# A 16-step ring in place of the 21-step tile loop of a fused cross-attention, self-attention and expert kernel

## The chip, the cores and the metric

The kernel runs on one core of a Trainium2 chip. The metric is the device time of one launch in microseconds (us). Five engines of the core have queues of their own and meet through semaphores: TensorE (PE in the profile), VectorE (DVE), ScalarE (ACT), GpSimd (POOL) and SyncE (SP), which here only issues transfers. Each engine works its queue strictly in the order in which the program wrote it, so an instruction that waits holds everything behind it on that engine.

## What is computed

The input x has 32 batches of 32 tokens with 256 features, and the context 32 batches of 257 rows with 64 features. Three layers follow each other, all in 32-bit accuracy:

```python
x = x + xattn(layernorm(x), ctx)      # 16 heads, softmax over 257 context rows, rotary embedding on ctx
x = x + attn(layernorm(x), wq, wk, wv, wo)   # 16 heads of 128, softmax over 32 tokens, block-scaled weights
x = x + ffn(layernorm(x))             # 64 experts, top 8 of them per token, at most 128 tokens each
```

## The kernel before

The 1024 tokens are cut into T = 8 tiles of 128 tokens, which are 4 batches each. The kernel has a fold stage (it multiplies the weights of the first layer together), the tile loop, and an expert stage. The change touches the tile loop alone.

**Three tiles at once.** In `tile(i, j, m)` the first layer runs for tile i ("X work"), the second for tile j = i - 1 ("S work"), and the output projection, the router and the scatter to the experts for m = j - 1. A tile has STEPS = 21 steps. ROWS = 16 of them each begin a "row": the scores of one batch and 4 heads (128 x 257, two f16 matmuls, L1188 and L1189, `score_row`). A row then passes through the negated maximum on VectorE (L830, `max_row`), the exponential on ScalarE (L609, `exp_row`), a transposition on TensorE two steps later (L1196, `transpose_row`), a copy on ScalarE (L617, `copy_row`) and the weighted sum on TensorE three steps later (L1207, `sum_row`). Scores have two PSUM banks, the transposed rows one, the sums of the RB = 4 rows of a batch share one. `normalise` on VectorE (L836 to L840) adds the part of context row 257, which GpSimd has prepared (L479, `last_rows`), and divides.

**Items between the rows.** The tables X_AT and BEHIND name what else stands in each step. X items: `hT` transposes the normalised tile, `qa` and `qb` make its queries (L1161; ScalarE casts them to f16 at L588, VectorE computes the f16 remainder at L824), `kt0` to `kt3` transpose the context of a batch (L1166, L592, L820), `cT0` to `cT3` transpose the normalised sums (L1171, L597), and `out` is the projection (L1175), which VectorE adds to X (L847). S items: `hT`, `q0` to `k3` (split f16 matmuls L1142 to L1144, drained by VectorE at L867), `sc` (scores, L1234; shifted on VectorE at L872 and L873, exponential on ScalarE at L638), `v0` to `v3` (drained by ScalarE, L630), `pv0` to `pv3` (L1244, drained at L634 and L883), `wo0` to `wo3`, `rT`, `log` and `pos`. Between `sc` and `pv0` lie the sum of the softmax (`softmax_sum`, L854), its end and transposition (`softmax_end`, L858 and L859) and four copies into a block-diagonal matrix on ScalarE (`spread`, L648). `chosen` (L903 to L907), `weigh` and `place` (L919 to L921) are the router's work on VectorE. The X items take turns on two PSUM banks, the S items on two others: an item may start when the item two places before it on the list XS or SS has been drained.

**The seam.** The rows fill steps 0 to 15. Steps 16 to 20 have no new row: they hold `qa`, `qb`, `cT3`, `kt0` and `out`, of which `qa`, `qb`, `kt0` belong to tile i + 1, and `score_row` of the next tile waits for `qb` and `kt0` before its first row. GpSimd runs a loop of its own: `rope_products` for tile i + 1 (L456 to L461), then for each batch `last_rows` and `rope_sums` (L471), and the scatter of tile m, 8 indirect transfers, at the end.

**The first tile** also carries 11 of the 16 parts in which the second layer's weights are dequantised (L769 on VectorE, L564 on ScalarE, L503 on GpSimd), in steps 0 to 15.

The order of the sums of a new batch is held by this line of `sum_row`, for the first row of the batch:

```python
e.wait_ge(on_ready, i * BT + b)      # normalise of the batch before has finished all three operations
```

## Time and profile before

| what | value |
|---|---|
| median of 3 runs | 779.98 us (776.14 to 783.31) |
| the profiled execution | 785.1 us, of which span 783.3 us |
| busy PE / DVE / ACT / POOL | 79% / 54% / 37% / 38% of the span |
| fold stage, until about | 78 us |
| tile loop | 78 to 629 us |
| expert stage | 629 to 783 us |

The profile is one execution. "Busy" counts the time in which an engine has an instruction in work; matmuls overlap, each is shown about 0.16 us longer than its place in the queue, so a short wait can hide in the busy time. "PEclk" is the granted clock of TensorE as a share of 2.4 GHz, 0.50 is 1.2 GHz. In the tables below, the stretches are cut where the projection `out` of a tile ends: 144.9 us for tile 0, then 199.9, 256.0, 317.6, 379.1, 440.6, 502.7 and 554.9 us.

### The profile page before, as it was taken

The numbers are of one execution on the slowest core, as the hardware profiler recorded it, in microseconds if no ns is written. First come the engines' busy times: TensorE is split into PE (matmuls) and PEld (weight loads), VectorE is DVE, ScalarE is ACT, GpSimd is POOL, SyncE is SP. The second block draws the span as 40 slices with busy tenths as digits, with TensorE's granted clock in tenths as the row PEclk, the third lists the DMA queues.
The fourth block names the chain that finished last, engine by engine and source line by source line (L and its number), as shares of the span: only waits on it lengthen the run. The fifth ranks groups of instructions, "written<-read, shape, count | busy, mean of one in ns | idle before, by whom it ended". The sixth has DMA issues, their size and how long they took to land.

```text
span 783.3 us, 16249 instructions
## 1 busy us (share of the span) xinstructions
PE 622.6 (79%) x6211; PEld 534.6 (68%) x6211; DVE 426.4 (54%) x1091; ACT 288.1 (37%) x798; POOL 294.7 (38%) x279
## 2 busy tenths in 40 slices
PE   6995677898999987898899798898874178898860
PEld 4884566797877876787787696796753067777750
DVE  1255485465676675676576577577653323333334
ACT  1123364337346345236236236246031033333320
POOL 3113299211214414313412412400303337777780
PEclk9975567999999999999999999999999579999995
DMA  7946993999001101100100200100101069999988
GB/s 200 293 140 156 237 251 84 294 338 300 6 2 53 38 3 54 35 3 34 55 3 18 72 2 2 69 2 2 66 2 51 28 167 284 301 301 296 303 168 275
DMA packets 98987, 97.61 MB, mean 125 GB/s; under 512 B 26238, under 2 KB 92848, under 8 KB 98912
## 3 DMA queue, kind: packets, MB, share of 16 engines
q1 hardware_dynamic: 86016, 78.21, 34.2%
q0 software_dynamic: 12288, 17.95, 10.5%
q8 instruction: 51, 0.84, 0.4%
q10 hardware_dynamic: 608, 0.42, 0.2%
q14 instruction: 24, 0.20, 0.1%
HBM read 62.32 MB, written 35.19 MB: 124 GB/s over the span
## 4 chain that ended last, share of the span: by engine, by line
PE 43%; DVE 20%; issue 13%; ACT 9%; POOL 6%; DMA 6%; another core or an unknown queue 2%; SPq 0%; POOLq 0%; DVEq 0%; PEldq 0%; ACTq 0%
POOL expert_sums L545 6%; PE bank L1161 5%; PE bank L1175 5%; PE bank L1142 5%; PE bank L1144 4%; PE bank L1143 4%; PE bank L1207 4%; DMA expert_sums<-Wh,etok 3%; PE bank L1244 3%; ACT pr L609 2%; DVE nmax L830 2%; PE bank L1196 2%; ACT diag L648 2%; ACT space L630 2%
## 5 line engine op out<-in xcount | busy, mean ns | idle before, releaser
L545 POOL DMA_INDIRECT expert_sums<-Wh,etok x64 | 98.8, 1544 | 37.8 <-issue 22.5
L609 ACT ACTIVATE pr<-bank,nmax 128x257 f32<-128x257 f32 x128 | 61.0, 477 | 101.4 <-DVE nmax L830 101.0
L1142 PE MATMUL bank<-space,Wh 128*128 128x128 f16 x512 | 88.3, 219 | 9.9 <-DVE X L928 7.1
L488 POOL DMA_INDIRECT expert_rows<-h,slot x64 | 62.7, 980 | 87.5 <-DVE slot L921 70.4
L1143 PE MATMUL bank<-space,Wh 128*128 128x128 f16 x512 | 88.2, 219 | 0.0
L1144 PE MATMUL bank<-space,Wl 128*128 128x128 f16 x512 | 88.2, 219 | 0.0
L1207 PE MATMUL bank<-Cr,pT 128*128 128x64 f32 x512 | 77.0, 276 | 9.4 <-DVE On L840 8.4
L471 POOL TENSOR_TENSOR Cr<-C,Ct 128x192 f32<-128x192 f32 x64 | 41.7, 675 | 104.9 <-PE bank L1207 104.8
L1207 PEld LDWEIGHTS bank<-Cr,pT 128*128 128x128 f32 x512 | 72.4, 204 | 12.4 <-issue 11.1
L830 DVE TENSOR_REDUCE nmax<-bank 128x1 f32<-128x257 f32 x128 | 53.3, 418 | 42.8 <-PE bank L1189 40.6
L479 POOL TENSOR_TENSOR On<-Cr,pr 128x256 f32<-128x256 f32 x32 | 20.7, 647 | 138.4 <-ACT pr L609 138.4
L1345 PE MATMUL bank<-Wh,ring 128*96 128x128 f32 x512 | 68.1, 277 | 0.0
L617 ACT COPY pT<-bank 128x256 f32<-128x256 f32 x128 | 47.6, 372 | 43.0 <-PE bank L1196 42.3
L1142 PE MATMUL bank<-Wh,space 128*128 128x256 f16 (+1 forms) x192 | 59.2, 309 | 4.8 <-ACT space L630 3.3
L867 DVE SCALAR_TENSOR_TENSOR space<-bank,bqk 128x512 f32<-128x512 f32 x64 | 43.5, 689 | 33.1 <-PE bank L1144 33.0
L1345 PEld LDWEIGHTS bank<-Wh,ring 128*96 128x96 f32 x512 | 60.9, 166 | 0.4 <-issue 0.3
L1196 PE MATMUL bank<-ident,pr 128*128 128x128 f32 x256 | 52.6, 289 | 10.5 <-ACT pT L617 10.5
L1142 PEld LDWEIGHTS bank<-space,Wh 128*128 128x128 f16 x512 | 51.1, 100 | 13.0 <-DVE X L928 8.2
L1143 PE MATMUL bank<-Wl,space 128*128 128x256 f16 (+1 forms) x192 | 59.1, 308 | 0.0
L1144 PE MATMUL bank<-Wh,space 128*128 128x256 f16 (+1 forms) x192 | 59.1, 308 | 0.0
L1354 PE MATMUL bank<-ring,Wh 96*128 96x256 f32 x128 | 43.4, 420 | 13.4 <-DVE Wh L1031 9.9
L1143 PEld LDWEIGHTS bank<-space,Wh 128*128 128x128 f16 x512 | 50.1, 98 | 0.1
(175 smaller groups left out, 1401.0 us busy)
## 6 DMA issues: line engine op xcount, KB each, us to landing
ring<-L_ffn_gate_up_proj_dram SPq DMA_DIRECT2D x64, 192.0 KB
expert_rows<-h SPq DMA_DIRECT2D x8, 1284.0 KB, 15.7
Wh<-expert_rows SPq DMA_DIRECT2D x64, 160.5 KB
ring<-L_ffn_down_proj_dram SPq DMA_DIRECT2D x64, 96.0 KB
expert_sums<-h SPq DMA_DIRECT2D x4, 1152.0 KB, 13.4
C<-ctx_dram SPq DMA_DIRECT2D x24, 128.0 KB, 3.3
Wl<-expert_sums SPq DMA_DIRECT2D x3, 1024.0 KB, 6.9
space<-L_xattn_Wo_dram SPq DMA_DIRECT2D x8, 256.0 KB, 4.8
```

The lines of the kernel that those rows point to most:

```text
L488: e.indirect_dma_start(XE[:, :], bass.IndirectOffsetOnAxis(ap=slot[:, k:k + 1], axis=0), h3[:, :], None, bounds_check=E * CAP - 1, oob_is_ ...
L545: e.indirect_dma_start(Y[n % NY][:, :], bass.IndirectOffsetOnAxis(ap=etok[:, n % 4:n % 4 + 1], axis=0), ye[:, n % 4], None, bounds_check=Y ...
L609: e.activation(pr[:, s, :], bank[r % 2][:, 0:NL], ACT.Exp, bias=nmax[:, s:s + 1], accum_out=rsum[:, s:s + 1]).then_inc(expd, 1)
L617: e.copy(pT[:, r % 2], bank[2][:, 0:2 * P].rearrange("p (c t) -> p c t", c=2)).then_inc(pt_ready, 1)
L830: e.tensor_reduce(nmax[:, s:s + 1], bank[r % 2][:, 0:NL], AX.X, ALU.max, negate=True).then_inc(maxed, 1)
L867: e.scalar_tensor_tensor((qS, kS)[w][:, 4 * g:4 * g + 4, :], src[:, :].rearrange("p (h t) -> p h t", h=4), 1.0 / WS, bqk[:, w, 4 * g:4 * g ...
L1142: e.matmul(dst, ah, bh, start=first and n == 0, stop=False)
L1143: e.matmul(dst, ah, bl, start=False, stop=False)
L1144: ins = e.matmul(dst, al, bh, start=False, stop=last and n == len(terms) - 1)
L1196: ins = e.transpose(bank[2][:, c * P:(c + 1) * P], pr[:, r % (2 * RB), c * P:(c + 1) * P], ident[:, :])
L1207: ins = e.matmul(bank[3][:, o:o + DC], pT[:, r % 2, c, :], Cr[:, b, c, 0, :], start=c == 0, stop=c == 1)
L1345: ins = e.matmul(bank[2 + n % 2][0:I, half * P:(half + 1) * P], gu[:, n, c, half * I:(half + 1) * I], xeT[:, n % 2, c, :], start=c == 0, s ...
```

## The change

The 21-step tile with its seam becomes a ring of 16 steps, in which a row starts in every step, over the tile border too. Step n = 16 g + t works on row t of tile g; there are 165 steps in all.

- **X items.** `hT`, `kt0`, `qa`, `qb` of tile g + 1 stand in steps 11, 12, 13 and 15 of tile g, in the order hT, kt0, qa, qb; `cT3` and `out` of tile g - 1 in steps 3 and 4 of tile g. `score_row` waits for `qa` before row 0 and for `qb` before row 2.
- **S items.** The S work of a tile begins in step 5 and ends in step 3 of the next turn. `wo0` and `wo1`, `q0` and `q1`, `q2` and `q3`, `pv0` and `pv1`, `pv2` and `pv3` share steps.
- **VectorE.** `chosen` stands behind the S item of its step (with `sc` in step 13, before it stood one step ahead of `sc`); `pos` stands behind `softmax_sum`, `place` ahead of the `pv` items.
- **sum_row.** The first row of each batch is issued at the end of its step, behind the X and S items, and waits only for the first addition of `normalise` (`x_link`), no longer for all three operations.
- **GpSimd.** `rope_products` stands in step 5, behind the scatter (step 4); the parts of tile 0 stand in the step of their number, the clearing of `diag` in step 9 of tile 1.
- **Waits moved.** VectorE's wait for the blanked expert rows (`own_tokens`) goes from the start of tile 2 to its step 10.

```diff
-XS = ["kt1", "kt2", "cT0", "kt3", "cT1", "cT2", "hT", "qa", "qb", "cT3", "kt0", "out"]
-X_AT = {2: ["kt1"], 6: ["kt2"], 7: ["cT0"], 10: ["kt3"], 11: ["cT1"], 15: ["cT2", "hT"], 16: ["qa"], 18: ["qb"],
-        19: ["cT3", "kt0"], 20: ["out"]}
+XS = ["kt1", "cT3", "out", "kt2", "cT0", "kt3", "cT1", "hT", "kt0", "qa", "qb", "cT2"]
+XTILE = {"cT3": -1, "out": -1, "hT": 1, "kt0": 1, "qa": 1, "qb": 1}
+X_AT = {2: ["kt1"], 3: ["cT3"], 4: ["out"], 6: ["kt2"], 7: ["cT0"], 10: ["kt3"], 11: ["cT1", "hT"], 12: ["kt0"],
+        13: ["qa"], 15: ["qb", "cT2"]}
...
-BEHIND = {0: ["wo0"], 1: ["wo1"], 2: ["wo2"], 3: ["hT", "wo3"], 4: ["q0"], 5: ["q1"], 6: ["q2", "q3"], 7: ["k0", "rT"],
-          8: ["k1", "k2", "log"], 9: ["k3"], 10: ["sc"], 11: ["v0", "pos"], 12: ["v1"], 13: ["v2"], 14: ["v3"],
-          15: ["pv0"], 16: ["pv1"], 17: ["pv2"], 18: ["pv3"]}
-STEPS = ROWS + 5
+S_FIRST = 5
+S_AT = {5: ["wo0", "wo1"], 6: ["wo2"], 7: ["hT", "wo3"], 8: ["q0", "q1"], 9: ["q2", "q3"], 10: ["k0"],
+        11: ["rT", "k1", "k2"], 12: ["log", "k3"], 13: ["sc"], 14: ["v0"], 15: ["pos", "v1"], 0: ["v2"], 1: ["v3"],
+        2: ["pv0", "pv1"], 3: ["pv2", "pv3"]}
+ALL_STEPS = ROWS * (T + 2) + S_FIRST
...
 # GpSimd
+            def step(g, t):
+                j, m = turn_of(g, t)
+                if t == 0 and 1 <= g <= T:
+                    last_rows(g - 1, 3)
+                if t == 3 and 1 <= g < T:
+                    rope_sums(g, 3)
+                if t == 4 and g < T:
+                    last_rows(g, 0)
+                if t == 4 and m is not None:
...
+                    scatter(m)
+                if t == 5 and g + 1 < T:
+                    rope_products(g + 1)
+                if t in (7, 11, 15) and g + 1 < T:
+                    rope_sums(g + 1, t // 4 - 1)
+                if t in (8, 12) and g < T:
+                    last_rows(g, t // 4 - 1)
...
 # VectorE
+            def step(g, t):
+                n = ROWS * g + t
+                j, m = turn_of(g, t)
+                if g < T:
+                    max_row(g, t)
+                if t % RB == 2 and RB + 2 <= n and n - RB - 2 < T * ROWS:
+                    normalise(*divmod((n - RB - 2) // RB, BT))
+                for name in X_AT.get(t, ()):
+                    if name in XSPLIT and 0 <= g + XTILE.get(name, 0) < T:
+                        x_low(name, g + XTILE.get(name, 0))
...
+                for name in S_AT.get(t, ()):
...
+                        s_use(name, j)
+                if j is not None and t == 14:
+                    softmax_sum(j)
+                if j is not None and t == 15:
+                    softmax_end(j)
+                if m is not None and t == 13:
+                    chosen(m)
...
 # TensorE, score_row and sum_row
-                if r == 0:
-                    wait_pos(e, xd, xpos("qb", i))
+                if r in (0, 2):
+                    wait_pos(e, xd, xpos("qb" if r else "qa", i))
...
-                if r % RB == 0:
-
-                    e.wait_ge(on_ready, i * BT + b)
+                if r % RB == 0 and i * BT + b >= 1:
+
+                    e.wait_ge(x_link, 2 * (i * BT + b) - 1)
...
+            def step(g, t):
+                if g < T:
+                    score_row(g, t)
+                row = row_of(ROWS * g + t - 2)
+                if row:
+                    transpose_row(*row)
+                row = row_of(ROWS * g + t - 3)
+                if row and row[1] % RB:
+                    sum_row(*row)
+                if g <= T:
+                    for name in X_AT.get(t, ()):
+                        x_item(name, g)
+                for name in S_AT.get(t, ()):
+                    s_item(name, *turn_of(g, t))
+                if row and row[1] % RB == 0:
+                    sum_row(*row)
```

**TensorE at the tile border.** Before, from `sum_row` of row 13 (step 16) to the first row of the next tile: L1161 is `qa` and `qb`, L1244 a `pv` item, L1171 `cT3`, L1166 `kt0`, L1175 `out`, L1188 the scores.

```order
L1207 MATMUL bank<-Cr,pT 128x64 x2
L1161 MATMUL bank<-h1T,M 128x128 x8
L1244 MATMUL bank<-diag,space 128x128 x4
L1196 MATMUL bank<-ident,pr 128x128 x2
L1207 MATMUL bank<-Cr,pT 128x64 x2
L1244 MATMUL bank<-diag,space 128x128 x4
L1207 MATMUL bank<-Cr,pT 128x64 x2
L1161 MATMUL bank<-h1T,M 128x128 x8
L1244 MATMUL bank<-diag,space 128x128 x4
L1171 MATMUL bank<-ident,On 128x128 x2
L1166 MATMUL bank<-ident,Cr 128x128 x3
L1175 MATMUL bank<-N,cT 128x256 x8
```

No scores stand in this stretch: it is the seam. After, steps 2 to 4 of the ring: L1151 is `kt1`, L1230 the `pv` items, L1156 `cT3`, L1160 `out`, L1174 and L1175 the scores, L1182 and L1193 transposition and sum.

```order
L1193 MATMUL bank<-Cr,pT 128x64 x2
L1151 MATMUL bank<-ident,Cr 128x128 x3
L1230 MATMUL bank<-diag,space 128x128 x8
L1174 MATMUL bank<-KTh,qspace 128x257
L1175 MATMUL bank<-KTl,qspace 128x257
L1182 MATMUL bank<-ident,pr 128x128 x2
L1156 MATMUL bank<-ident,On 128x128 x2
L1230 MATMUL bank<-diag,space 128x128 x8
L1193 MATMUL bank<-Cr,pT 128x64 x2
L1174 MATMUL bank<-KTh,qspace 128x257
L1175 MATMUL bank<-KTl,qspace 128x257
L1182 MATMUL bank<-ident,pr 128x128 x2
```

The queries and `kt0` have left this place, rows have come in, and the first sum of the batch (the last L1193) stands behind the `pv` items.

**VectorE between the scores of the S work and its softmax.** Before, from `sc` (L872) to the end of the softmax (L859); L830 is a row's maximum, L896 to L899 `pos`.

```order
L872 TENSOR_REDUCE smax<-bank 128x16
L873 TENSOR_TENSOR space<-bank,smax 128x512
L830 TENSOR_REDUCE nmax<-bank 128x1
L896 TENSOR_TENSOR sv<-bank,slot 128x64
L897 SCALAR_TENSOR_TENSOR sv<-bank,sv 128x64
L899 TENSOR_TENSOR count<-count,mask 128x64
L854 TENSOR_REDUCE ssum<-space 128x16
L855 RECIPROCAL sinv<-ssum 128x16
L830 TENSOR_REDUCE nmax<-bank 128x1
L858 TENSOR_TENSOR space<-space,sinv 128x512
L859 STREAM_TRANSPOSE space<-space 128x512
```

Only a row's maximum and `pos` stand between `sc` and the sum. After, from the remainder of `qa` (L819) through `sc` (L867, L868), `chosen` (L898 to L902), a row's maximum (L825), `normalise` (L831 to L835) and `softmax_sum` (L849, L850) to the next row's maximum:

```order
L819 TENSOR_TENSOR qspace<-bank,qspace 64x4x4x32 x2
L867 TENSOR_REDUCE smax<-bank 128x16
L868 TENSOR_TENSOR space<-bank,smax 128x512
L898 CAST topf<-topi 128x8
L899 TENSOR_TENSOR space<-iota_e,topf 128x512
L902 TENSOR_REDUCE mask<-space 128x64
L825 TENSOR_REDUCE nmax<-bank 128x1
L831 TENSOR_TENSOR On<-bank,On 128x256
L834 RECIPROCAL rinv<-rsum 128x4
L835 TENSOR_TENSOR On<-On,rinv 128x256
L849 TENSOR_REDUCE ssum<-space 128x16
L850 RECIPROCAL sinv<-ssum 128x16
```

Behind these rows follow the remainder of `qb` (L819), `pos` (L891 to L894), and only then the end of the softmax (L853, L854).

## Rows read from the trace of the kernel before

**Rows 1.** Busy time by stretches, us: PE, PEld, DVE, ACT, POOL, clock, DMA

```profile
145.00:199.90 54.90, 51.22 (x627) 45.34 (x625) 32.26 (x72) 26.26 (x75) 12.20 (x17) 1.00 0.92 297
199.90:256.00 56.10, 51.60 (x634) 45.60 (x633) 38.91 (x102) 27.42 (x79) 16.57 (x20) 1.00 0.06 22
256.00:317.60 61.60, 53.73 (x635) 46.47 (x633) 39.58 (x102) 27.14 (x79) 20.30 (x26) 0.97 0.12 36
440.60:502.70 62.10, 53.72 (x635) 46.86 (x633) 41.44 (x102) 27.22 (x79) 19.05 (x23) 0.97 0.07 25
502.70:554.90 52.20, 47.40 (x597) 41.60 (x596) 34.68 (x96) 24.53 (x73) 7.49 (x10) 1.00 0.04 14
```

**Rows 2.** Waits of PE from 379.1 to 440.6: us, times, longest

```profile
PE bank L1166 <- DVE qspace L824: 2.5, 1, 2.5
PE bank L1207 <- DVE On L840: 1.3, 1, 1.3
PE bank L1142 <- DVE X L928: 1.3, 1, 1.3
PE bank L1220 <- DVE h L811: 1.1, 1, 1.1
```

**Rows 3.** Stretches at the seam, columns as in rows 1

```profile
250.00:256.00 6.00, 4.42 (x25) 3.61 (x24) 2.50 (x4) 1.78 (x4) 4.74 (x5) 1.00 0.38 140
370.00:374.00 4.00, 1.29 (x9) 0.84 (x8) 2.07 (x3) 1.71 (x4) 3.08 (x4) 1.00 0.36 134
375.00:376.00 1.00, 1.00 (x4) 0.77 (x3) 0.43 (x1) 0.01 (x1) 0.98 (x2) 0.50 0.45 164
```

**Rows 4.** Timeline of PE, items: start, us, [idle before]

```profile
252.32 3.69 PE L1175 MATMUL bank<-N,cT 128*128 128x256 f32 x16
...
367.35 2.00 PE L1161 MATMUL bank<-h1T,M 128*128 128x128 f32 x16
...
373.73 5.38 PE L1175 MATMUL bank<-N,cT 128*128 128x256 f32 x16 [0.94 <-issue]
```

**Rows 5.** Timeline of DVE, operations of one step each

```profile
408.07 1.10 DVE L907 TENSOR_REDUCE mask<-space 128x64 bf16<-128x512 f32 x1
...
409.55 0.41 DVE L836 TENSOR_TENSOR On<-bank,On 128x256 f32<-128x256 f32 x1
...
410.89 0.68 DVE L872 TENSOR_REDUCE smax<-bank 128x16 f32<-128x512 f32 x1
...
413.77 0.69 DVE L854 TENSOR_REDUCE ssum<-space 128x16 f32<-128x512 f32 x1
...
414.77 0.42 DVE L830 TENSOR_REDUCE nmax<-bank 128x1 f32<-128x257 f32 x1
...
426.93 1.39 DVE L824 TENSOR_TENSOR qspace<-bank,qspace 64x512 f16<-64x512 f32 x2 [0.82 <-ACT qspace L588]
```

**Rows 6.** Timeline of ACT, operations of one step each

```profile
417.36 1.24 ACT L648 COPY diag<-space 32x512 f32<-32x512 f32 x2
418.62 0.60 ACT L630 ACTIVATE space<-bank 128x512 f32<-128x512 f32 x1
...
425.73 1.17 ACT L588 CAST qspace<-bank 64x512 f16<-64x512 f32 x2 [1.59 <-PE bank L1161]
```

**Rows 7.** Timeline of DVE: one operation of the norm's chain, in two tiles

```profile
204.30 0.16 DVE L744 TENSOR_TENSOR rs<-rs 128x1 f32<-128x1 f32 x1
...
384.23 1.35 DVE L744 TENSOR_TENSOR rs<-rs 128x1 f32<-128x1 f32 x1
```

**Rows 8.** Timeline of POOL at that time

```profile
383.76 1.81 POOL L461 TENSOR_TENSOR C<-C,cosT 128x768 f32<-128x768 f32 x1
```

**Rows 9.** Timeline of PE at the start of tile 0

```profile
78.65 6.64 PE L1161 MATMUL bank<-h1T,M 128*128 128x128 f32 x32 [0.55 <-ACT h1T L597]
87.98 0.91 PE L1166 MATMUL bank<-ident,Cr 128*128 128x128 f32 x3 [2.69 <-DVE qspace L824]
89.81 0.40 PE L1188 MATMUL bank<-KTh,qspace 128*128 128x257 f16 x1 [0.93 <-DVE KTl L820]
```

More of the change, by code:

```diff
@@ L692, in expert_copy @@
+            e.sem_inc(x_high, XSPLIT.index("kt0"))
+            for name in XS:
+                if XTILE.get(name, 0) == 1:
+                    x_use(name, 0)
+            for n in range(ALL_STEPS):
+                step(n // ROWS, n % ROWS)
             def expert_copy(ex, n):
@@ L1011, in _ @@
             next_h1(0)
-            for name in ("qa", "qb", "kt0"):
-                x_low(name, 0)
-            tile(0, None, None)
-            tile(1, 0, None)
-            e.wait_ge(zero_out, 16 * (E // 8 + NY))
-            e.tensor_scalar(h3[:, D + E:ROW], h3[:, D + E:ROW], float(-(B * S + P)), None, ALU.add).then_inc(zeroed, 1)
-            e.wait_ge(zeroed, 3)
-            for j in range(1, T - 2):
-                tile(j + 1, j, j - 1)
-            tile(T - 1, T - 2, T - 3, last=True)
-            tile(None, T - 1, T - 2)
-            tile(None, None, T - 1)
+            for name in XSPLIT:
+                if XTILE.get(name, 0) == 1:
+                    x_low(name, 0)
+            for n in range(ALL_STEPS):
+                step(n // ROWS, n % ROWS)
+            assert all(done[which, i] == count for which, count in (("x", XLINKS), ("s", SLINKS), ("r", RLINKS))
+                       for i in range(T)), done
             def experts(j, first):
@@ L1322, in _, with x_item @@
-            for name in XS:
-                (x_use(name, 0) if name in XNEXT else x_skip(name, -1))
-            tile(0, None, None)
-            tile(1, 0, None)
-            for j in range(1, T - 2):
-                tile(j + 1, j, j - 1)
-            tile(T - 1, T - 2, T - 3, last=True)
-            tile(None, T - 1, T - 2)
-            tile(None, None, T - 1)
+            def x_item(name, g):
+                i = g + XTILE.get(name, 0)
+                if 0 <= i < T:
+                    x_use(name, i)
+                else:
+                    x_skip(name, i)
@@ L1333, in expert_t @@
+            for name in XS:
+                x_item(name, -1)
+            for n in range(ALL_STEPS):
+                step(n // ROWS, n % ROWS)
             def expert_t(j, n):
```

251 lines of the change are left out of this document (99 added, 152 removed).

## The prediction

> **What bounds the kernel now.** I read the page first: TensorE is busy 79% of the span, no other engine over 54%. Then the busy time by stretches, cut where `out` of a tile ends [rows 1]. Tiles 3 to 6 take 61.6, 61.5, 61.5 and 62.1 us, 246.7 together, and TensorE is busy for 53.7 of each. Tile 2 has the same work (634 matmul records against 635) and takes 56.1, with 51.6 busy. So a full tile is bound by TensorE's queue with 51.6 us of work, plus what it waits, plus something that makes the same work 2.1 us longer. The waits of a steady tile are the third view [rows 2]: 2.5 us for the remainder of the queries, 1.3 for the division of the batch before, 1.3 for X, 1.1 for h; four short ones, 1.6 us together, bring it to 7.8, as 61.5 - 53.7 asks. The longer work is the clock: at the seam TensorE idles 2.7 us of 370 to 374, and at 375 it is granted 0.50, which is 1.2 GHz [rows 3]. The sixteen matmul records of `out` then take 5.38 us instead of 3.69 (which holds `kt0` too) [rows 4]. I count 1.8 us a tile. In tile 2 it idles 1.6 us at this place and the clock stays 1.00 [rows 3].
>
> By the Trainium skill (TensorE: Matmul & The Clock Gate, HAM oscillation) a TensorE that pauses too long is put back to half its clock and pays for it at the next burst. The trace agrees: 0.50 right behind the gap.
>
> **What the ring takes away.** The 2.5 us for the query remainder and the pause before `out` go: `qa` and `qb` stand in steps 13 and 15 and are wanted in steps 0 and 2, several us of TensorE work later; `cT3` and `out` have two `pv` items and a sum between them. The 1.3 us for the division go: the first sum stands behind the items and waits for one operation of three. With the gap at the seam the fall of the clock there goes, 1.8 us.
>
> **What it adds.** No instruction of weight is added. The order is what changes, so I walk one period with the rows' durations, TensorE's own pieces being scores 0.22, transposition 0.22, sum 0.39, query item 1.84, `sc` 1.2, a `v` item 1.3 (starts of neighbours in the timeline). The bad place is `sc`. Behind the last matmul of `qa` (time 0) come, each waiting for the one before: cast of `qa` on ScalarE 1.2 [rows 6], its remainder on VectorE 1.3, as the queue is in order [rows 5]: 2.5. Only then maximum and shift of `sc`, 2 x 0.7: 3.9. `chosen`, 0.2 + 0.7 + 1.1: 6.0. Row maximum and `normalise`, 0.35 + 1.0: 7.4. `softmax_sum`, 1.0: 8.4. The maximum of row 15, its exponential and the cast of `qb` on ScalarE, 0.35 + 0.5 + 1.2: 10.5. Its remainder 1.3, `pos` 0.7, the end of the softmax 1.4: 13.9. Maximum and exponential of row 0, 0.9, then ScalarE's queue: two pairs of `spread` at 1.25, `v2` 0.5, the copy of row 15 0.25, exponential 0.5, `v3` 0.6 [rows 6]: 19.2 when `pv0` may start. TensorE has in that time `sc` 1.2, steps 14, 15, 0 and 1 with 2.1 + 4.3 + 2.1 + 2.1, and 1.2 of step 2: 13.0. So 6.2 us of waits lie between `qa` and `pv0`, in five pieces: the transposition of row 13 for the copy of row 12, which stands behind the exponential of `sc` (1.6), `cT2` (0.4), `v2` for `pos` (2.0), the transposition of row 0 (1.0), `pv0` (1.2). Before, none of `qa`, `qb`, `chosen` stood in this chain.
>
> The rest of the period: `hT` of the S work. From the end of `out` VectorE does a maximum, X and its norm (3.5 us), then `normalise` and the remainder of `kt2`, then the second half of the norm: h is there at 7.5, TensorE at 6.6: 1.0. The first `q` waits for X 0.8 (before 1.3), `rT` and `k` 1.4 together, since `self_out_norm` now stands behind `normalise`. Sum 6.2 + 3.2 = 9.4. The profile hides 0.16 us of each of the eight, so it would show 8.2 idle. Then GpSimd: the same small product of the norm takes 0.16 us in one tile and 1.35 in another [rows 7], where it ends with the GpSimd operation beside it [rows 8]. In the ring `rope_products` comes behind ten us of scatter, about 6 to 10 us behind `out`, again on the second half of that norm. I take 0.5. The two bounds are 0 and the 1.2 us of the rows.
>
> The Trainium skill (GPSIMD Engine Reference, Specifications) says that VectorE and GpSimd share an SBUF interface when VectorE reads two SBUF tensors. By that the product can be held each time it meets a `rope` operation, 1.2 us in every tile and the sum below 4 us dearer. The trace shows both cases.
>
> **The sum, against the profiled 783.3 us.** A full tile of the ring: 51.6 + 8.2 + 0.5 = 60.3 us.
> - Tiles 3 to 6: 4 x 60.3 = 241.2 against 246.7: -5.5.
> - Tile 2: 59.8 (its `rope_products` is early, as now) against 56.1: +3.7. It never lost its clock.
> - Tile 1 has no router work; without `chosen` and `pos` the chain is 2.9 us shorter. 51.2 busy, idle 3.7: 54.9, as now: 0.
> - Tile 7 has no queries to make and 5 of its 16 rows have moved ahead (0.83 each, 4.2 us): 47.4 - 4.2 + 6.7 idle (3.2 as above, 3.5 around `sc`) = 49.9 against 52.2: -2.3.
> - Tile 0: `kt0` before the queries. Now it waits 2.69 us behind them and the first row starts at 89.8 [rows 9]; in the new order the 32 records of the queries end at 85.3 and row 0 can go: -4. At its end the five rows that moved in fill the seam but GpSimd, behind which the last batch stands, is busy with parts: +1. Together -3.
> - Behind tile 7 the order is the same but for `chosen` and `place`: 0. Expert stage: 0.
>
> Sum -7.1. The profiled execution took 785.1 us, the median is 780.0; I set the change against the median: 773.
>
> **Rivals.**
> A (forecast, 0.42): as above, 768 to 778.
> B: the clock falls at the new gaps (0.2). In step 2 TensorE works 0.2, waits 1.0, works 0.9, waits 1.2; that is less idle than the 2.7 us behind which it fell and more than tile 2's 1.6, behind which it did not [rows 3]. One fall costs 1.8 in each of tiles 2 to 6, 9 us: 782, no change.
> C: the ring is better than my walk (0.25). Each wait rests on a chain of ten durations, and if VectorE gets `chosen` or `normalise` done while ScalarE casts, two us a tile go in tiles 1 to 6, -12: 761. For it: VectorE is busy only 41 of 62 us [rows 1]. Against it: its queue is in order and `qa`'s remainder waits at its head.
> D: slower (0.13). The clock falls twice in a period, at `v2` and at `pv0`, 3.6 us in each of tiles 2 to 6, and GpSimd's hold is the full 1.2: 18 + 3 - 7 = +14: 794. It decides the case if two gaps of a period are each followed by a granted clock of 0.50; with one of them it is B.
>
> The rule of the page cited first is what B and D rest on: by it the time would be 782 or 794. The trace so far bears it out at the seam alone.
>
> **How the numbers follow.** About 1% is what a measurement of this kernel tells from no change, 772 to 788. A lies across the lower bound: I give a third of it to faster. Faster: 0.14 + 0.24 (C) = 0.38. Slower: D, 0.12 with a bit of B, 0.15. Same 0.47. The range reaches from C, 761, with 3 us below it, to the end of B: 758 to 787. It leaves out D and the far end of C, 2 in 10.
>
> **What the profile after would show.** Right: steady tiles near 60 us; no wait for the query remainder before `kt0`; no wait of the weighted sum for the division; `out` in 3.7 us at clock 1.00; new waits of `v2`, `pv0` and row transpositions of 1 to 2 us each; first row near 85.5 us; tile 2 longer than 56.1. Wrong: tiles of 57 or less (then the chain behind `qa` is shorter than walked), 0.50 in the clock behind step 0 or 2 (B, D), or a wait of GpSimd's `last_rows` behind the scatter, which I cost at nothing since `normalise` of batch 1 comes 8 us later.

## The result and the profile after

The changed kernel takes 828.6 us (819.8 to 830.2, 4 runs) beside 781.6 us (776.1 to 789.1, 4 runs) of the kernel before: ratio 1.060, 95% interval 1.049 to 1.072. A second timing gave 827.6 beside 780.0, ratio 1.056 (1.046 to 1.066). The forecast was 773, with a range to 787. The profiled execution took 830.0 us (span 828.1); it is set against the 783.3 us of the trace before.

By stretches, cut where `out` ends as before (150.7, 213.3, 274.6, 342.4, 409.9, 477.5, 544.4, 601.8 us):

| stretch | before | after | forecast |
|---|---|---|---|
| to the end of tile 0 | 145.0 | 150.7 | 142.0 |
| tile 1 | 54.9 | 62.6 | 54.9 |
| tile 2 | 56.1 | 61.3 | 59.8 |
| tiles 3 to 6, each | 61.5 to 62.0 | 66.9 to 67.8 | 60.3 |
| tile 7 | 52.3 | 57.3 | 49.9 |
| the rest, to the end | 228.4 | 226.4 | 228.4 |

The busy time of three of them (columns as in [rows 1]), tiles 1, 2 and 5:

```profile
150.70:213.30 62.60, 53.74 (x627) 47.38 (x625) 34.07 (x71) 26.60 (x75) 15.68 (x19) 0.95 0.85 271
213.30:274.60 61.30, 51.91 (x635) 45.69 (x633) 39.80 (x103) 27.19 (x79) 10.72 (x16) 1.00 0.05 13
409.90:477.50 67.60, 56.91 (x635) 48.43 (x633) 40.60 (x102) 27.14 (x79) 18.70 (x24) 0.92 0.08 27
```

Tile 2 is the ring as I walked it, 51.9 busy and 9.4 idle at full clock. Tile 5 has the same work and a scatter besides, is 6.3 us longer, and runs at 0.92. TensorE's waits in tile 5, against [rows 2]:

```profile
PE bank L1206 <- DVE h L806: 2.7, 2, 1.7
PE bank L1156 <- DVE On L835: 2.0, 2, 1.8
PE bank L1127 <- DVE sv L892: 1.9, 1, 1.9
PE bank L1182 <- ACT pT L624: 1.7, 1, 1.7
PE bank L1230 <- ACT space L637: 0.8, 1, 0.8
```

The waits at the seam are gone. The last three of these are those walked (1.9 for `pos`, 1.7 for the copy of row 12, 0.8 before `pv0`). The longer ones of the first two, 1.7 for h and 1.8 for `cT0`, lie 8 to 12 us behind `out`, and there something else happens. ScalarE, then VectorE, then the transposition on TensorE that the copy L624 waits for, in the order of time:

```profile
411.05 0.20 ACT L616 ACTIVATION_READ_ACCUMULATOR pr<-bank,nmax 128x1 f32 x1
417.33 0.37 ACT L624 COPY pT<-bank 128x256 f32<-128x256 f32 x1 [6.08 <-remote]
```
```profile
412.75 0.16 DVE L736 SCALAR_TENSOR_TENSOR rs<-rs 128x1 f32<-128x1 f32 x1
417.37 0.43 DVE L825 TENSOR_REDUCE nmax<-bank 128x1 f32<-128x257 f32 x1 [4.46 <-remote]
417.71 0.42 DVE L831 TENSOR_TENSOR On<-bank,On 128x256 f32<-128x256 f32 x1
418.16 0.18 DVE L834 RECIPROCAL rinv<-rsum 128x4 f32<-128x4 f32 x1
418.37 1.51 DVE L835 TENSOR_TENSOR On<-On,rinv 128x256 f32<-128x256 f32 x1
```
```profile
413.44 0.38 PE L1182 MATMUL bank<-ident,pr 128*128 128x128 f32 x2
```

Both stand still and go on within 0.04 us of each other. "Remote" says that the profile shows nobody who released them. Not all of the 6.08 and 4.46 us is the stop: ScalarE could not copy before the transposition ended at 413.8, VectorE could not take the maximum before the scores ended at 413.6. In tile 2 the same copy waits 2.6 us for TensorE and starts 0.04 us behind the transposition:

```profile
216.85 0.38 PE L1182 MATMUL bank<-ident,pr 128*128 128x128 f32 x2
217.27 0.37 ACT L624 COPY pT<-bank 128x256 f32<-128x256 f32 x1 [2.61 <-PE bank L1182]
```

In tile 5 it starts 3.5 us behind it, and the maximum 3.8 us behind its scores (0.1 in tile 2). That is the stop. In tiles 3 to 7 it is 3.4 to 3.7 us on ScalarE and 3.7 to 3.9 on VectorE. GpSimd at that time, first and last of the eight transfers and what follows:

```profile
405.80 1.01 POOL L500 DMA_INDIRECT expert_rows<-h,slot  x1 [0.18 <-issue]
...
414.78 0.97 POOL L500 DMA_INDIRECT expert_rows<-h,slot  x1 [0.30 <-issue]
415.77 1.00 POOL L468 TENSOR_TENSOR Ct<-C,sinT 128x384 f32<-128x384 f32 x1
416.71 1.00 POOL L470 TENSOR_TENSOR Ct<-C,sinT 128x384 f32<-128x384 f32 x1
417.79 1.80 POOL L473 TENSOR_TENSOR C<-C,cosT 128x768 f32<-128x768 f32 x1
```

Here the stop ends about when the scatter's data has landed (its last packets start at 416.9). The division L835, which takes 0.42 us in tile 7, where no rope operation runs, and 0.85 in tile 2, takes 1.51 beside `rope_products`. TensorE then:

```profile
418.00:422.00 4.00, 0.67 (x4) 0.22 (x3) 3.75 (x11) 0.93 (x4) 2.80 (x3) 0.88 0.00 0
422.00:426.00 4.00, 3.82 (x19) 3.11 (x20) 0.79 (x3) 1.10 (x4) 0.62 (x1) 0.50 0.00 0
```

It works 0.67 of 4 us and is then granted 0.50, 1.2 GHz. ScalarE's wait of 6.0 to 6.2 us, with the stop in it, stands in each of tiles 3 to 7, the five that have a scatter under rows, and not in tile 2. It is no wait for instructions to arrive, as far as the trace tells: no packet of the instruction queues starts between 410.2 and 430.5.

### The profile page after: what moved, and what is told of

Its sections match the earlier page's. It is cut to its first block, busy times and chain, and to the rows that moved or that the text cites. A ratio compares the mean times of both kernels' runs of the same rounds, so it can differ in the third digit from the quotient of the medians.

```text
span 828.1 us, 16290 instructions
## 1 busy us (share of the span) xinstructions
PE 641.5 (77%) x6211; PEld 544.4 (66%) x6211; DVE 428.8 (52%) x1091; ACT 287.8 (35%) x798; POOL 292.3 (35%) x279
## 4 chain that ended last, share of the span: by engine, by line
PE 42%; DVE 23%; issue 12%; ACT 7%; DMA 7%; POOL 6%; another core or an unknown queue 2%; SPq 0%; POOLq 0%; DVEq 0%; PEldq 0%; ACTq 0%
PE bank L1127 5%; PE bank L1129 5%; PE bank L1128 5%; DMA expert_sums<-Wh,etok 4%; POOL expert_sums L557 4%; PE bank L1193 4%; PE bank L1160 4%; PE bank L1230 3%; DVE qspace L819 2%; PE bank L1146 2%; DVE On L835 2%; ACT qspace L600 2%; PE bank L1116 2%; PE bank L1104 2%
## 5 line engine op out<-in xcount | busy, mean ns | idle before, releaser
L483 POOL TENSOR_TENSOR Cr<-C,Ct 128x192 f32<-128x192 f32 x64 | 38.4, 622 | 180.3 <-PE bank L1193 175.9
L624 ACT COPY pT<-bank 128x256 f32<-128x256 f32 x128 | 47.6, 372 | 148.4 <-PE bank L1182 117.5
L1127 PE MATMUL bank<-space,Wh 128*128 128x128 f16 x512 | 90.1, 222 | 7.3 <-DVE obias L932 2.7
L616 ACT ACTIVATE pr<-bank,nmax 128x257 f32<-128x257 f32 x128 | 61.1, 477 | 84.8 <-DVE nmax L825 83.9
L1128 PE MATMUL bank<-space,Wh 128*128 128x128 f16 x512 | 89.8, 221 | 0.0
L825 DVE TENSOR_REDUCE nmax<-bank 128x1 f32<-128x257 f32 x128 | 53.2, 418 | 68.4 <-PE bank L1175 49.6
L1193 PE MATMUL bank<-Cr,pT 128*128 128x64 f32 x512 | 79.3, 282 | 0.0
L1193 PEld LDWEIGHTS bank<-Cr,pT 128*128 128x128 f32 x512 | 77.0, 214 | 1.7 <-issue 0.3
L1182 PE MATMUL bank<-ident,pr 128*128 128x128 f32 x256 | 54.0, 296 | 29.6 <-ACT pT L624 29.3
L1127 PE MATMUL bank<-Wh,space 128*128 128x256 f16 (+1 forms) x192 | 64.1, 334 | 13.5 <-DVE sv L892 9.3
L1334 PE MATMUL bank<-Wh,ring 128*96 128x128 f32 x512 | 67.7, 276 | 0.1
L1129 PE MATMUL bank<-Wh,space 128*128 128x256 f16 (+1 forms) x192 | 64.7, 337 | 1.5 <-issue 1.5
L1128 PE MATMUL bank<-Wl,space 128*128 128x256 f16 (+1 forms) x192 | 64.5, 336 | 1.7 <-issue 1.7
L1334 PEld LDWEIGHTS bank<-Wh,ring 128*96 128x96 f32 x512 | 60.6, 166 | 0.6 <-issue 0.5
L1182 PEld LDWEIGHTS bank<-ident,pr 128*128 128x128 f32 x256 | 33.7, 153 | 39.2 <-issue 37.2
L1127 PEld LDWEIGHTS bank<-space,Wh 128*128 128x128 f16 x512 | 51.4, 100 | 11.4 <-DVE X L923 3.4
## 6 DMA issues: line engine op xcount, KB each, us to landing
expert_rows<-h SPq DMA_DIRECT2D x8, 1284.0 KB, 15.6
```

The lines of the kernel that those rows point to most:

```text
L616: e.activation(pr[:, s, :], bank[r % 2][:, 0:NL], ACT.Exp, bias=nmax[:, s:s + 1], accum_out=rsum[:, s:s + 1]).then_inc(expd, 1)
L624: e.copy(pT[:, r % 2], bank[2][:, 0:2 * P].rearrange("p (c t) -> p c t", c=2)).then_inc(pt_ready, 1)
L825: e.tensor_reduce(nmax[:, s:s + 1], bank[r % 2][:, 0:NL], AX.X, ALU.max, negate=True).then_inc(maxed, 1)
L1127: e.matmul(dst, ah, bh, start=first and n == 0, stop=False)
L1128: e.matmul(dst, ah, bl, start=False, stop=False)
L1129: ins = e.matmul(dst, al, bh, start=False, stop=last and n == len(terms) - 1)
```

## Experiments

The last two columns are of the profiled execution: the mean of tiles 3 to 6, and from the end of tile 7 to the end. "Before" is the kernel before in the same comparison. A row without a ratio is a single execution.

| label | us | before | ratio | tiles 3-6 | rest |
|---|---|---|---|---|---|
| before | 781.6 | | | 61.7 | 228.4 |
| after | 828.6 | 781.6 | 1.060 | 67.5 | 226.4 |
| ring_no_scatter | 779.5 | 785.3 | 0.993 | 61.1 | 212.6 |
| before_no_scatter | 749.8 | 785.3 | 0.955 | 56.3 | 212.8 |
| ring_half_scatter | 787.2 | 785.3 | | 61.2 | 221.8 |
| ring_early_scatter | 811.0 | 785.3 | 1.039 | 63.9 | 226.6 |
| ring_split_scatter | 794.4 | 764.9 | 1.039 | 61.2 | 223.3 |
| ring_paired_scatter | 785.4 | 764.9 | | 61.1 | 226.3 |
| ring_plain_scatter | 785.0 | 764.9 | | 61.1 | 219.6 |
| before_split_scatter | 767.3 | 764.9 | 1.005 | 57.9 | 224.2 |
| before_again | 777.8 | 780.0 | | 60.0 | 230.1 |
| ring_again | 827.6 | 780.0 | 1.056 | 67.6 | 229.3 |
| ring_short_chain | 799.5 | 780.0 | 1.013 | 59.9 | 225.8 |
| before_split_sum | 782.7 | 780.0 | 1.001 | 59.7 | 228.6 |
| ring_shorter_chain | 774.8 | 759.8 | 1.023 | 58.9 | 227.0 |
| ring_paired_again | 792.6 | 759.8 | 1.047 | 61.1 | 226.2 |
| before_split_again | 768.0 | 759.8 | 1.015 | 57.5 | 225.0 |
| ring_six_scatter | 799.3 | 759.8 | | 64.0 | 223.0 |
| before_third | 763.9 | 768.4 | | 56.4 | 228.0 |
| before_paired_scatter | 762.0 | 768.4 | 1.001 | 56.9 | 225.6 |

The kernel before is itself near 782 us in three of the comparisons and near 764 in the other three. So times are only read beside their own "before", and tiles from the traces. The number of the chip does not tell the two kinds apart: the record has chip 13 both at 764.9 and at 780.0.

**1. The scatter left out.** In `scatter` (shortened here; the waits for the scatter's end go too), and with `range(4)` and `range(6)` in place of the cut in the half and the six one:

```
-                for k in range(TOPK):
-                    e.indirect_dma_start(XE[:, :], ..., h3[:, :], ...).then_inc(scat, 16)
```

> The changed kernel with the eight indirect transfers of each scatter left out, so the expert stage reads blanked rows; all waits on the scatter's end are gone, everything else stands. Theory S (the scatter under the rows is what makes the ring slow: ScalarE, VectorE and TensorE resume together at 417.3 us when its data has landed, TensorE then drops to 0.50): tiles 3 to 6 fall from 67.5 us to the 61.2 of tile 2, which has no scatter, tile 7 from 57.4 to about 53, about 30 us in all: near 798 us. Theory Q (the queues' order alone makes the tile long: the chain behind qa and the norm, with or without the scatter): tiles 3 to 6 stay above 65, the kernel above 815 us. Rival C (it is only the clock that falls): tiles about 64, TensorE's granted clock 1.00 in place of 0.92 to 0.97, and the wait of ScalarE for the row's transposition still there at 6 us.

> The kernel before with the same eight transfers left out: what the scatter costs behind the seam. Theory S: it cost something there too, less, since at the seam only out and kt0 stand in its way: tiles 3 to 6 fall from 61.6 us towards the 56.1 of tile 2, at most 5.5 each, so between 755 us (all of it) and 775 us. If S is wrong (tile 2 is short for want of its router transfers' neighbours, not of the scatter): within 1% of before, 782. The difference of ring and before without any scatter is the cost of the ring proper: by my walk it should be near 0; what is left of the 47 us is then not the scatter's.

> The changed kernel with four of the eight transfers of each scatter left out (half of the chosen experts get no row). Tells whether the stall has the length of the scatter. Theory S with a stall that lasts until the scatter's data has landed: the three engines resume near 412 us in the frame of the full kernel, 5 us sooner, before or just as VectorE comes to the second half of the norm, and the stall of ScalarE shrinks from 6 us to about 1; tiles 3 to 6 near 62 to 63. If the stall hangs on something that only begins at the fourth or fifth transfer or on the first one alone: 6 us as before, tiles at 67, or none.

> The changed kernel with two of the eight transfers of each scatter left out. With four a steady tile took 61.3 us, with eight 67.5. If each transfer behind the fourth costs the same, because the other engines stand still while it runs: 64.4. If there is a threshold at five (one stall of fixed length, until the data of all has landed): the stall ends 2.5 us sooner, 65. If it is only the last two: 61.3.

Without a scatter the ring's tiles 3 to 6 are all 61.1 us, those of the kernel before 56.3. Theory S holds for what the scatter costs under the rows: 6.4 us a tile, 5.7 in tile 7. Behind the loop it costs 13.8 in the ring and 15.6 before, which no expectation had, so both times came out lower than expected (779.5 for 798, 749.8 for 755 to 775). Theory Q holds for the rest, since the ring is still 4.8 us a tile longer than before without any scatter, and 29.7 us longer as a whole (1.040). So the scatter is not the main part of the change's loss: it cost the kernel before 5.4 us a tile as well, and of the 5.8 us by which the ring's tiles 3 to 6 are longer, 4.8 are there without it. Rival C falls: here is a tile of 61.0 at a clock of 0.97, as long as tile 2 at 1.00; the ring waits for its chain, and a fall of the clock is paid out of waiting.

```profile
207.10:268.30 61.20, 51.81 (x634) 45.59 (x633) 39.80 (x103) 27.21 (x79) 10.75 (x15) 1.00 0.03 8
390.50:451.50 61.00, 53.28 (x634) 46.30 (x633) 39.75 (x102) 27.21 (x79) 10.16 (x15) 0.97 0.03 8
```

Four transfers cost nothing in the tiles. Six cost 2.9 us, near the 64.4 of a price for each transfer, but not by a stop: ScalarE's copy starts 0.04 us behind its transposition in every tile. (This was run where the kernel before took 760, see 3.) `rope_products` comes two transfers sooner and meets the norm's first half; this is VectorE in `ring_six_scatter`, with GpSimd's last transfer and `rope_products`:

```profile
399.24 0.27 DVE L734 TENSOR_SCALAR rs<-rs,mv 128x1 f32<-128x1 f32 x1
399.55 2.46 DVE L736 SCALAR_TENSOR_TENSOR rs<-rs 128x1 f32<-128x1 f32 x1
...
403.05 1.10 DVE L835 TENSOR_TENSOR On<-On,rinv 128x256 f32<-128x256 f32 x1
...
404.41 0.26 DVE L734 TENSOR_SCALAR rs<-rs,mv 128x1 f32<-128x1 f32 x1
404.70 0.46 DVE L736 SCALAR_TENSOR_TENSOR rs<-rs 128x1 f32<-128x1 f32 x1
```
```profile
399.03 0.97 POOL L500 DMA_INDIRECT expert_rows<-h,slot  x1 [0.30 <-issue]
400.00 1.03 POOL L468 TENSOR_TENSOR Ct<-C,sinT 128x384 f32<-128x384 f32 x1
400.95 1.03 POOL L470 TENSOR_TENSOR Ct<-C,sinT 128x384 f32<-128x384 f32 x1
402.06 1.81 POOL L473 TENSOR_TENSOR C<-C,cosT 128x768 f32<-128x768 f32 x1
403.95 1.19 POOL L483 TENSOR_TENSOR Cr<-C,Ct 128x192 f32<-128x192 f32 x2
```

L736, 0.16 elsewhere, took 2.46 and ended with the second operation of `rope_products`; L835 took 1.10 where tile 2 of the ring has 0.85. Part of that time is spent waiting anyway: h is 1.9 us later behind `out` than without a scatter (9.6 for 7.7). Tile 6, at full clock, is 1.8 us longer; the other three lie at 0.95 to 0.97 and are 2.9 to 3.5 longer. Beside L483 the instruction L734, whose operands in SBUF are one tensor and a column of factors, keeps its 0.26 while L736 behind it takes 0.46. The trace agrees there with the Trainium skill (GPSIMD Engine Reference, Specifications), which has the shared interface contended by VectorE instructions with two SBUF inputs.

**2. The scatter in other places.** Early: the step of `scatter` is 3, ahead of `last_rows`, in place of 4. Split and paired (`turn` is the tile of step 4):

```
-                if t == 4 and m is not None: scatter(m)
+                if t == 3: scatter(m, range(0, 4))      # split;  paired: range(0, 2)
+                                                        #         paired: t == 4, behind last_rows: range(2, 4)
+                if t == 6: scatter(turn, range(4, 8))   # split;  paired: range(4, 6), and t == 7: range(6, 8)
```

The code is shortened; the last tile's second half is issued behind the loop. Plain: each `indirect_dma_start` is a `dma_start` of `h3` to 128 consecutive rows.

> The changed kernel, all of its work, with the scatter in GpSimd's queue in step 3 ahead of last_rows, where it now stands in step 4 behind it: it begins at about 401 us in place of 405.8 and its data has landed by 412.5. Theory S: the stall moves to 408 to 412, behind out, where VectorE has X and its norm to do from PSUM that is already filled; rope_products end at 415 in place of 419.6 and no longer meet the norm's second half. 2 to 4 us per tile less in tiles 3 to 7, 10 to 20 in all: 810 to 818 us. Theory Q: the same time within 0.5%, or slower, as last_rows of batch 0 now comes 5 us later. Rival: the stall costs the same wherever the rows run beside it: 828.

> The changed kernel, all of its work, with each scatter cut in two: four transfers in step 3, ahead of last_rows, and four in step 6, behind rope_products, so that GpSimd does about 5 us of other work between them. Without a scatter a steady tile took 61.06 us, with four transfers 61.3, with eight 67.5: the first four cost 0.2, the next four 6.2. Theory B (a backlog: the stall comes only when more than four or five transfers follow each other): both halves are free, tiles 3 to 6 at 61.3 to 62, 785 to 792 us. Theory P (place: what stalls is what TensorE does 5 us and more after batch 1 has begun, whoever is running; the second half lies in that place, about 5 to 10 us later than in the full kernel): tiles at 65 to 67, 810 to 828 us.

> As the split one, but in pairs: two transfers each in step 3, step 4 behind last_rows, step 6 behind rope_products and step 7 behind rope_sums, with 0.6 to 4 us of GpSimd's other work between them, eight transfers within some 19 us. Theory B with a backlog that drains between pairs: tiles at 61.3, as with four transfers. If the backlog is counted over a longer time than these gaps give, or if the price is one of the transfers' number: tiles at 64 to 67.

> The changed kernel with each of the eight indirect transfers replaced by a plain one on the same queue, in the same place, that writes the same 128 rows of 1284 bytes to consecutive places (so the rows land at the wrong experts). It tells the bytes from the way they are addressed. If it is the bytes, or the number of transfers in the queue, that stalls the other engines: ScalarE still waits 6 us for the transposition, tiles 3 to 6 at 66 to 68. If it is the work of GpSimd on the rows' addresses, or the scattered writes: no such wait, tiles at 61 to 62.5, below 795 us.

Early gains 3.5 us a tile, within what S expected, and "remote" waits of 0.9 to 3 us on ScalarE move with the scatter. Split, paired and plain are at 60.9 to 61.4 in all of tiles 3 to 6, as if there were no scatter. That fits theory B, a backlog of more than four indirect transfers in a row, and a cost that is not one of bytes. It doesn't show either: these three, and the six transfers of 1, were run where the kernel before took 760 to 765, and the next section shows that the stop can be absent there anyway. What speaks for B in comparisons that did have the stop are `ring_half_scatter` (a single execution) and, below, the pairs of `ring_short_chain` and the halves of `before_split_sum`: none shows it in tiles 3 to 6. For plain transfers, and for six, there is no such run.

**3. The two kernels again.**

> The kernel before, unchanged, for a trace of its own beside the next three. In the last comparison it took 764.9 us where it had taken 785.3 in the one before, and before_split_scatter was no faster than it. Two readings: the stall behind the scatter differs from chip to chip (then the tiles 3 to 6 here are 57 to 58 us where the time is near 765, 61.5 where it is near 782, and the waits of ScalarE at the seam are there only in the second case), or the whole execution was quicker, the fold and expert stages too, with tiles of 61.5 all the same.

> The changed kernel, unchanged. If the stall is there in this comparison (before near 782): tiles 3 to 6 at 67.5 and 828 us, ratio 1.06. If it is not (before near 765): tiles at 61.1 to 61.5, about 787, and the ratio is that of the ring proper, 1.03. If the stall comes with the ring alone and the kernel before was only quicker by chance: 828 beside 765.

> The kernel before, unchanged. Its time was near 782 us in three comparisons and near 762 in two others, and no trace is at hand from the second kind. If this one is of the second kind (below 770) its trace shows where the 20 us are: tiles 3 to 6 at 57 us with TensorE's clock at 1.00 and the scatter all the same (then the stall at the seam is what differs), or tiles as long as in the first traces and shorter fold and expert stages. If it is near 780 it adds nothing but a third set of tiles: 58 to 61.6.

`ring_again` repeats the first trace: 67.5, 67.5, 67.5 and 67.7, with the same 6.1 us on ScalarE. `before_third` is the key to my mistake. It has the seam and eight transfers in one piece, and its tiles 3 to 6 take 56.7, 56.0, 56.3 and 56.7. The seam in it:

```profile
362.83 0.38 PE L1171 MATMUL bank<-ident,On 128*128 128x128 f32 x2
364.78 0.44 PE L1166 MATMUL bank<-ident,Cr 128*128 128x128 f32 x2 [1.57 <-DVE qspace L824]
...
365.17 3.62 PE L1175 MATMUL bank<-N,cT 128*128 128x256 f32 x16
```
```profile
362.70:366.70 4.00, 2.43 (x16) 2.01 (x15) 2.50 (x4) 1.83 (x5) 3.08 (x4) 1.00 0.36 132
366.70:370.70 4.00, 4.00 (x29) 3.46 (x28) 1.18 (x3) 0.56 (x2) 2.79 (x4) 1.00 0.31 114
```

And the same place in the trace of [rows 3, 4], where `out` took 5.38 us:

```profile
372.48 0.58 ACT L634 CAST space<-bank 128x512 f16<-128x512 f32 x1 [1.72 <-remote]
373.21 0.37 ACT L597 COPY cT<-bank 128x256 f32<-128x256 f32 x1
374.64 0.38 ACT L592 CAST KTh<-bank 128x257 f16<-128x257 f32 x1 [1.05 <-remote]
```

The same instructions in the same order, with GpSimd's transfers at the same place; only where ScalarE is stopped does TensorE's pause grow from 1.6 to 2.7 us and the clock fall. So the 5 us by which tiles 3 to 6 exceeded tile 2 before were the scatter's stop and the clock behind it, and not what the seam costs alone. The stop is a different one here: two, of 1.7 and 1.1 us, and the second ends at 374.6, while the scatter still has 96 packets to go, so the landing of the data is not what ends it. And a seam whose own pause is longer can lose the clock with no scatter at all. This is the seam of tile 0 in `before_third`, before the first scatter, and the clock is 0.73 from 140.0 to 145.3:

```profile
139.79 0.90 PE L1166 MATMUL bank<-ident,Cr 128*128 128x128 f32 x3 [2.41 <-DVE qspace L824]
140.48 4.82 PE L1175 MATMUL bank<-N,cT 128*128 128x256 f32 x16
```

In `before_no_scatter` the same wait, 2.39, is followed by an `out` of 3.62 at clock 1.00: a pause of that length can be followed by either.

**4. The chain behind `qa`.** VectorE's queue in steps 12 to 15, on the paired ring:

```
 step 12:  log, k3                                      + chosen            (shorter)
 step 13:  maximum, qa's remainder, sc, chosen          -> maximum, sc, qa's remainder
 step 14:  ..., softmax_sum                             + chosen            (short)
 step 15:  maximum, qb's remainder, pos, softmax_end    -> maximum, softmax_end, pos, qb's remainder
```

> All of the ring's work, the scatter in pairs as in ring_paired_scatter (steady tiles 61.1 us, 9.2 of them idle), and VectorE's queue behind qa in another order: the scores' maximum and shift ahead of qa's remainder, chosen behind softmax_sum, softmax_end ahead of pos and of qb's remainder. By the walk of the prediction the end of the softmax comes 3.7 us sooner and pv0 could start 15.5 us behind qa in place of 19.2, with 13 us of TensorE work between. Theory Q (this chain is the price of the ring over before, 61.1 against 56.0 to 57.6 us): tiles 57.5 to 58.5, waits for the copy of row 12, for pos and before pv0 together under 3 us in place of 6. If the idle time is only passed on (the queries' remainder now late for row 0, or chosen late for pos): 60 to 61.

> ring_short_chain with chosen one step further ahead, at the end of step 12, in the 2.8 us that VectorE spends waiting for the cast of qa. In ring_short_chain a steady tile took 59.5 us and the 3.6 us of waits for pos and the copy of row 12 had become 2.5 us for chosen's mask. Theory Q (the chain behind qa is the ring's price): that wait goes as well, 0 to 0.5 is left of it, tiles 57 to 57.7, about 12 us less than ring_short_chain over tiles 2 to 7 and 20 less than ring_paired_scatter. Rival (the idle time goes round: TensorE waits for whoever is last, and pv0 or h takes it up): 59 to 59.5, with pv0's wait at 3 us or more.

> The changed kernel with its scatter in pairs, timed in rounds, since the one look at it came from a comparison in which the kernel before took 764.9 us. By the traces (61.1 in place of 67.5 in tiles 3 to 6, 50.5 in place of 57.4 in tile 7) it is 30 to 33 us faster than the ring with the scatter in one piece: a ratio to before of 1.01 to 1.025, against 1.056 and 1.060.

`ring_short_chain`: 59.4 to 59.6 in three of the tiles 3 to 6 and 61.1 in one, in place of 61.1, where 57.5 to 58.5 had been expected; the waits for `pos` and for the copy of row 12 were replaced by 2.5 us for `chosen`. `ring_shorter_chain` takes that away too and has a tile as expected, 57.4 at full clock; the next three take 60.3, 59.0 and 58.8, with the clock at 0.94, 0.97 and 0.97:

```profile
262.40:319.80 57.40, 51.57 (x634) 45.53 (x633) 39.78 (x102) 27.16 (x79) 18.62 (x24) 1.00 0.10 31
319.80:380.10 60.30, 54.47 (x635) 48.41 (x633) 39.87 (x102) 27.55 (x79) 19.70 (x25) 0.94 0.09 30
```

Busy time differs by 2.9, length by 2.9: now that the chain no longer binds, the clock is paid in full. The whole kernel takes 0.976 of `ring_paired_again` (1.0225 against 1.0474), 18 us. (That one missed its own expectation of 1.01 to 1.025: its time of 792.6 is 35 us under the ring's 828, but the kernel before took 760 beside it.) The chain was the ring's price over before, theory Q; of the 3.7 us that it gives back a tile, the clock takes 1.5 on the mean.

**5. The kernel before with parts of it.** In `before_split_scatter` four transfers stay where the scatter stands now, behind `last_rows` of batch 3, and four go behind `rope_products` of the next tile; `before_paired_scatter` has two each at four places around the rope operations. `before_split_sum` is the sum's half of the change on `before_split_scatter`: the first sum behind the items, waiting for `x_link`.

> The kernel before, all of its work, with the same cut: four transfers where the scatter stands now, behind last_rows of batch 3, four behind rope_products of the next tile. The kernel before without any scatter took 749.8 us against 785.3, tiles 3 to 6 56.0 against 61.6. Theory B: both halves are free, tiles 3 to 6 at 56 to 57.5, four tiles at least 4 us shorter each, 17 to 22 us in the loop: 763 to 769 us; the two scatters behind the loop stay whole. Theory P: the same as before within 1%.

> The kernel before with its scatter in two halves, a second time beside another set of runs of before. Traces: its tiles 3 to 6 took 58.5, 57.7, 57.6 and 57.6, those of before 61.6, 61.5, 61.5 and 62.1 in one trace and 60.5, 58.0, 61.0 and 60.4 in another, with TensorE's clock at 0.94 to 0.97 where they are long and 1.00 where they are short. If the scatter in one piece costs the kernel before its clock each tile: 3 us a tile, ratio 0.98 to 0.985. If the ratio 1.005 of the first comparison holds, the fall of the clock at the seam depends on the execution, and the halved scatter is worth nothing here: 0.995 to 1.01.

> The second half of the change alone, on before_split_scatter (tiles 57.6 us, of which 1.3 is the first sum's wait for all of normalise): the first sum of each batch stands at the end of its step and waits for one operation of three. If the wait is real: one wait of 1.3 us a tile is gone and the shorter ones of the other batches too, tiles 56.2 to 57, 5 to 10 us less in all than before_split_scatter. If VectorE or ScalarE takes it up, or the sum is now late for the copy of the next row: within 3 us of it.

> The kernel before, all of its work, with the scatter in pairs around the rope operations: two transfers, rope_sums of batch 3, two, rope_products of the next tile, two, last_rows of batch 0, two. In before_split_scatter rope_products ran 1.5 to 2 us behind out, into the norm, and last_rows of batch 0 waited 3.9 us for the landing of the scatter; tiles 57.6 us against 56.0 without a scatter. In pairs rope_products starts 2.5 us sooner and nothing waits for the landing until later: tiles 56.0 to 57, 4 to 8 us less than before_split_scatter, 757 to 762 us, and faster than before by 0.5 to 3% according to which kind of comparison this is. If the transfers themselves, not their order, hold up the norm: 57.6 again, 766.

Halves and pairs gained nothing: 1.005 (interval 1.001 to 1.009) and 1.015 (1.008 to 1.022) for the halves, both above 1 by their intervals, and 1.001 (0.995 to 1.008) for the pairs, where a gain of 0.5 to 3% had been expected. Where before is near 764 it has no stop to take away, and in `before_split_scatter` the halves put `rope_products` 1.5 to 2 us behind `out` and let `last_rows` wait 3.9 us for the landing. The one comparison with the stop (780) had `before_split_sum`. Its tiles 3 to 6 took 61.5, 58.3, 58.3 and 60.6 in an execution of 786 us. The first and last fell in the clock at the seam, `out` took 5.31, with no "remote" wait beside them. I read the two at clock 1.00: 0.7 more than the halves alone. The sum's wait is gone, and `cT3` (L1175 there) waits as long for the same division, a step later:

```profile
PE bank L1170 <- DVE qspace L828: 1.9, 1, 1.9
PE bank L1146 <- DVE X L932: 1.6, 1, 1.6
PE bank L1175 <- DVE On L844: 1.3, 1, 1.3
```

The rival held: the second half of the change gains nothing by itself. No version here that does all the work beats the kernel before beyond its interval.

## Why the prediction was wrong

The traces differ by 44.9 us where the sum said -7.1. The 52 us between are: tiles 3 to 6 28.6, tile 7 7.5, tile 1 7.7, tile 2 1.4, tile 0 8.7, the rest -2.0.

- **The scatter under the rows was costed at nothing, and with it the sum of tiles 3 to 6 failed.** I had 61.5 against 56.1 for the same work, put the difference down to the seam's waits and the fall of the clock behind them ("with the gap at the seam the fall of the clock there goes"), and let the ring take both away. `before_no_scatter` and `before_third` have the seam and take 56.0 to 56.7. The difference belonged to the scatter, which the ring keeps and moves from under `out` to under the rows and the norm. There it costs 6.4 a tile, 25.6 of the 28.6. h is ready 12.1 us behind the end of `out` in place of 7.7 without a scatter: 4.4, of which 3.7 is VectorE's stop and the rest GpSimd's hold. The other 2.0 is what remains, and TensorE restarts at 0.50 there. I costed "a wait of GpSimd's `last_rows` behind the scatter" at nothing and looked no further at what runs beside it, though the trace before showed "remote" waits of ScalarE at each seam with a scatter.
- **The walk of the ring was right.** 60.3 forecast, 61.1 measured without the stop; 59.8 forecast and 61.3 measured in tile 2. In tile 5 of the trace after, the transposition of row 13 waits 1.7 (1.6), `v2` 1.9 (2.0), `pv0` 0.8 (1.2). `ring_shorter_chain` shows its parts can be taken away one by one, 3.7 us in all.
- **But its comparison was wrong.** Against 56.3 of a kernel before without the stop, the ring's waits cost 4.8 a tile, and that is most of what the change loses in tiles 3 to 6. I read that only for tile 2 (+3.7, measured +5.1).
- **Tile 1, "the chain is 2.9 us shorter: 54.9, as now", failed.** It took 62.6, and 62.4 without any scatter. Its waits after:

```profile
PE bank L1127 <- DVE obias L932: 2.7, 1, 2.7
PE bank L1220 <- issue: 2.1, 1, 2.1
PE bank L1206 <- DVE h L806: 1.8, 1, 1.8
```

 With 1.3 and 1.0 more before `pv0` and a transposition it idles 8.9. I had 3.7: `obias_out`, which the change puts in step 8 of VectorE's queue, is in no term of my sum, and the clock is 0.95. Without a scatter the wait for `obias_out` is 0.4 and the one for h 3.3, in a tile as long. Which of them sets the length, and why `sc` starts 2.1 late, was not tried.
- **Tile 0: the first half held, "the five rows fill the seam" failed.** From the transposition of h to the first row it is 8.0 us after and 12.4 before, the 4 us forecast; the start of the loop was later in this execution, at 81.6 in place of 77.4. But from the first row to the end of `out` it is 61.1 us after and 55.2 before. TensorE waits 15.7 us there for ScalarE's copies of the rows (9.4 before), so it is not TensorE's work that sets the pace of this tile, and the stretch costs 6 in place of my 1. That it is the rows in steps 16 to 19, or the parts of the weights, that set it was not tested.
- **`out` in 3.7 us at clock 1.00 held**, as did the end of the two seam waits. **GpSimd's hold, 0.5 with bounds 0 and 1.2:** in tiles 3 to 6 L835 is 1.0 to 1.3 us longer than alone and L736 0.3, 1.3 to 1.6 together, of which 0.4 stands in tile 2 too; tile 7, with no rope operation, has none. `ring_six_scatter` has 2.3 on one instruction. The bound taken from one row was no bound.
- **Rivals.** D had the right sign and a clock of 0.50, but at another gap and for a cause it did not name; its 794 is 35 us short. B's fall at the chain's gaps is seen in `ring_no_scatter` and costs nothing while the chain binds.

**What stays open.** Why eight indirect transfers in a row stop engines that do not wait for them, and why the kernel before shows it in two traces and not in a third. The transfers look the same in all (1.32 MB in 384 packets of one queue). Whether it takes more than four of them, or more than six, or needs them indirect, is argued and not shown. Whether the ring with its scatter in one piece is also quicker where before takes 764 was not tried.

## What to carry to other kernels

When two tiles with the same instructions differ in length, first name what runs beside the longer one, and take it out on its own; a gap that is seen at a place need not belong to that place. In this kernel a ring without a seam could pay only if the chains that the seam had kept apart (here the queries' casts and the softmax of the other tile, on one VectorE queue in order) still fit into TensorE's work. A fall of the clock costs its time only where TensorE bounds the stretch.

## What the runs showed of the hardware

- While eight indirect transfers issued by GpSimd in one piece (1.28 us each) ran beside the ring's rows, ScalarE started 3.4 to 3.7 us and VectorE 3.7 to 3.9 us after the TensorE work that they wait for had ended (0.04 and 0.11 without), in tiles 3 to 7 of `after` and of `ring_again`; both went on 11.5 to 11.6 us after the first transfer. Four in a row and pairs showed no such stop in tiles 3 to 6, nor did eight plain ones of the same bytes (these only where the kernel before took 765). The kernel before showed shorter ones on ScalarE, 0.8 to 2.0 us each, in two of three traces and none in the third.
- An operation of VectorE on two SBUF tensors of one element a partition took 2.46 us in place of 0.16 beside the last transfer and two GpSimd operations behind it; one with a single tensor and a column of factors kept its 0.26 beside another GpSimd operation.
- The same wait of TensorE, 2.4 us, was followed by a granted clock of 0.73 and an `out` of 4.82 us in one execution, and by 1.00 and 3.62 in another.
